# A macaron block on one core: the mixer chain split at the convolution, with four hid buffers and routing operands in PSUM

## The reference

```python
x = x + 0.5 * ffn(layernorm(x))
x = x + mixer(layernorm(x))
x = x + 0.5 * ffn(layernorm(x))       # the same weights as the first
```

## Time and profile before

| | us |
|---|---|
| median of 3 runs | 724.22 (724.0 to 727.43) |
| the profiled execution | 724.26 |
| its span, first to last instruction | 722.5 |
| PE busy / DVE busy / POOL busy / ACT busy | 668.6 / 580.9 / 480.9 / 420.2 |
| mean granted TensorE clock | 0.989 |

### The profile page before, as it was taken

The page is one execution under the profiler, slowest core; times in us unless marked ns, Lnnn a source line. Parts: engine busy times, 40 slices in busy tenths (PEclk is TensorE's granted clock), DMA queues, the critical chain, the costliest instruction groups (busy, mean ns, idle before and its releaser), DMA issues. The chain is left out here.

```text
span 722.5 us, 10391 instructions
## 1 busy us (share of the span) xinstructions
PE 668.6 (93%) x3016; PEld 524.4 (73%) x3016; DVE 580.9 (80%) x1543; ACT 420.2 (58%) x801; POOL 480.9 (67%) x714
## 2 busy tenths in 40 slices
PE   6589998988987999999999999999999899999996
PEld 5468776776766887767777787776778677777784
DVE  5787797788978788887897969988788887978663
ACT  4446655664665656566566565655665655665553
POOL 1147657765677766777567775777667776686775
PEclk9899999999999999999999999999999999999999
DMA  8492908308373290925719074461907346190550
GB/s 196 99 205 70 198 1 191 62 5 194 70 168 75 57 216 4 198 55 113 154 46 192 15 178 89 105 133 45 216 7 167 85 99 139 41 196 16 126 128 15
DMA packets 59994, 78.84 MB, mean 109 GB/s; under 512 B 7680, under 2 KB 27168, under 8 KB 59936
## 3 DMA queue, kind: packets, MB, share of 16 engines
q1 hardware_dynamic: 59408, 77.91, 49.8%
q10 hardware_dynamic: 528, 0.26, 0.2%
HBM read 75.01 MB, written 3.15 MB: 108 GB/s over the span
## 5 line engine op out<-in xcount | busy, mean ns | idle before, releaser
L479 POOL TENSOR_TENSOR hid_lo<-hid,hid_hi 128x256 fp32r<-128x256 f32 x544 | 392.1, 743 | 200.7 <-ACT hid_hi L576 200.0
L576 ACT ACTIVATE hid_hi<-hid 128x512 fp32r<-128x512 f32 x272 | 170.5, 627 | 118.5 <-DVE hid L725 117.3
L712 DVE TENSOR_TENSOR weighted<-gate_ps,raw 128x512 f32<-128x512 f32 x256 | 175.4, 685 | 68.7 <-ACT gate_ps L568 55.8
L568 ACT ACTIVATE gate_ps<-gate_ps 128x512 f32<-128x512 f32 x256 | 148.6, 580 | 105.5 <-PE gate_ps L982 103.0
L725 DVE TENSOR_TENSOR hid<-weighted,up_ps 128x512 f32<-128x512 f32 x256 | 174.8, 683 | 13.8 <-DVE weighted L712 0.5
L1025 PE MATMUL down_ps<-hid_hi,wt_hi 128*128 128x512 f32 x272 | 108.7, 400 | 6.7 <-ACT ffn_sb L580 6.7
L1028 PE MATMUL down_ps<-hid_lo,wt_hi 128*128 128x512 f32 x272 | 108.2, 398 | 0.8 <-POOL hid_lo L479 0.7
L1026 PE MATMUL down_ps<-hid_hi,wt_lo 128*128 128x512 f32 x272 | 107.9, 397 | 0.0
L980 PE MATMUL up_ps<-xT_hi,wt_hi 128*128 128x512 f32 x187 | 78.1, 417 | 12.5 <-DVE hid L725 12.2
L980 PE MATMUL gate_ps<-xT_hi,wt_hi 128*128 128x512 f32 x187 | 80.6, 431 | 4.1 <-DVE weighted L712 3.9
L982 PE MATMUL gate_ps<-xT_hi,wt_lo 128*128 128x512 f32 x187 | 74.8, 400 | 0.0
(11 more groups left out here) (140 smaller groups left out, 1082.7 us busy)
## 6 DMA issues: line engine op xcount, KB each, us to landing
raw<-wT_hbm SPq DMA_DIRECT2D x64, 640.0 KB, 13.3
raw<-wT_hbm SPq DMA_DIRECT2D x32, 512.0 KB, 7.7
raw<-wT_hbm SPq DMA_DIRECT2D x32, 256.0 KB, 3.9
x_res<-in_L_attn_x SPq DMA_DIRECT2D x8, 256.0 KB, 5.6
out_x<-x SPq DMA_DIRECT2D x8, 256.0 KB, 2.3
x_ln<-in_L_attn_x SPq DMA_DIRECT2D x7, 256.0 KB, 14.1
raw<-in_L_ffn_gate_w SPq DMA_DIRECT2D x4, 256.0 KB, 5.3
raw<-in_L_ffn_up_w SPq DMA_DIRECT2D x4, 256.0 KB, 4.9
```

The source lines that it names most:

```text
L479: last = nc.gpsimd.tensor_tensor(hid_lo[s][:, cols], hid[s][:, cols], hid_hi[s][:, cols].bitcast(F32), ALU.subtract)
L568: nc.scalar.activation(bank[:, :] if j else silu_sb[:, :], bank[:, :], ACT.Silu).then_inc(silu_done, 1)
L576: nc.scalar.activation(hid_hi[s][:, :], hid[s][:, :], ACT.Copy).then_inc(hid_hi_done, 1)
L712: V.tensor_tensor(weighted[j % 2][:, :], gate_ps[n % BANKS][:, :], wb[:, j - 1, :], ALU.mult)\
```

## The change

The ring of hid buffers gets a fourth member. Five small operands of the routing (16 columns each) are placed in free columns of the PSUM bank `routed`, where five others are already. The slot tables are redrawn: the chain is cut before the convolution. A unit (4, b) now carries layer norms 3 and 4 of block b+1 (`NORM4`), the chain of block b+2 up to the value's copy (`PROJECT`) and the first router of block b+3 (`PREPARE`). A unit (1, b) carries the convolution, recurrence and output projection of block b-1 (`MIXER`), the transpose and the second router of block b-2 (`XT4`, `ROUTE4`) and the output of block b-3. Stats and layer norm 1 of the next block (`NEXT`) come two to two and a half slots later, and the weights of both routers one slot later. PE issues down of tile 0 at slot 4 together with down of tile 1, instead of at slot 3. The tanh of the gate waits until the mixer's work on the block before is done.

```diff
--- before.py
+++ after.py
@@ -42,7 +42,7 @@
 
 ORDER = [(1, 0), (1, 1), (1, 2)] + [f for b in range(NBLK - 3) for f in ((4, b), (1, b + 3))]
 ORDER += [(4, NBLK - 3), (4, NBLK - 2), (4, NBLK - 1)]
-RING = 3
+RING = 4
 BANKS = 2
 NBATCH = 14
 
@@ -201,15 +201,15 @@
         best1 = sb("best1", [P, TT * NG])
         is_best = sb("is_best", [P, TT, E])
         others = sb("others", [P, TT, E])
-        n_best = sb("n_best", [P, TT * NG])
-        far_single = sb("far_single", [P, TT * NG])
+        n_best = routed[:, 388:388 + TT * NG]
+        far_single = routed[:, 404:404 + TT * NG]
         best1_tied = sb("best1_tied", [P, TT * NG])
-        best_other = sb("best_other", [P, TT * NG])
-        best2 = sb("best2", [P, TT * NG])
+        best_other = routed[:, 420:420 + TT * NG]
+        best2 = routed[:, 436:436 + TT * NG]
         gsum = sb("gsum", [P, TT, NG])
         gdiff = sb("gdiff", [P, TT, NG * NG])
         beats = sb("beats", [P, TT * NG, NG])
-        grank = sb("grank", [P, TT * NG])
+        grank = routed[:, 452:452 + TT * NG]
         gmask = sb("gmask", [P, TT * NG], I32)
         masked = sb("masked", [P, TT, E + TOP])
         top8 = sb("top8", [P, TT, 8])
@@ -286,40 +286,44 @@
         FIRST = {"norm 1": 0, "normalise 1": 0, "transpose 1": 2, "xT high 1": 2, "xT low 1": 2.5, "router 1": 3,
                  "logits 1": 3.5, "silu logits 1": 4, "route 1": (4.5, 5, 5.5, 6, 6.5, 7, 7.5, 8, 9, 9.5, 10),
                  "weights 1": 12}
-        NEXT = {"stats 1": 11.5, "meanvar 1": 12, "norm 1": 13, "normalise 1": 14}
+        NEXT = {"stats 1": 14, "meanvar 1": 14.5, "norm 1": 15, "normalise 1": 16}
         PREPARE = {"transpose 1": 1, "xT high 1": 1, "xT low 1": 1.5, "router 1": 2, "logits 1": 2.5,
-                   "silu logits 1": 3, "route 1": (4, 4.5, 5.5, 6, 6.5, 7, 8, 8.5, 9, 9.5, 10), "weights 1": 12}
-        CHAIN = {"copy ffn 1": 2, "transpose ffn 1": 3, "add ffn 1": 3.5, "stats 2": 4, "meanvar 2": 4,
-                 "norm 2": 4, "normalise 2": 5, "add ln_b": 9, "transpose 2": 7, "xT high 2": 7,
-                 "xT low 2": 7.5, "mixer gate": 9, "tanh gate": 9, "mixer value": 10, "copy value": 10,
-                 "conv": (11, 11.5, 12, 12.5, 13, 13.5), "y high": 14, "y low": 14,
-                 "mixer out": 16, "mixer sum": 16.5}
-        NORM4 = {"stats 3": 0, "meanvar 3": 0.5, "norm 3": 1, "normalise 3": 2, "scale 3": 3, "x2": 4.5, "stats 4": 5,
-                 "meanvar 4": 5, "norm 4": 6, "normalise 4": 7, "transpose 4": 14, "xT high 4": 14, "xT low 4": 14.5}
-        ROUTE4 = {"router 4": 1, "logits 4": 1.5, "silu logits 4": 2,
-                  "route 4": (2.5, 3.5, 5.5, 6, 6.5, 7, 8, 8.5, 9, 9.5, 10.5), "weights 4": 12}
+                   "silu logits 1": 3, "route 1": (4.5, 5, 5.5, 6.5, 7, 8, 8.5, 9.5, 10.5, 11, 12), "weights 1": 13}
+
+        PROJECT = {"copy ffn 1": 2, "transpose ffn 1": 3, "add ffn 1": 3.5, "stats 2": 4, "meanvar 2": 4,
+                   "norm 2": 4, "normalise 2": 5, "transpose 2": 7, "xT high 2": 7, "xT low 2": 7.5,
+                   "mixer gate": 9, "tanh gate": 9, "mixer value": 10, "copy value": 10, "add ln_b": 15}
+        MIXER = {"conv": (0, 0.5, 1, 2, 3, 3.5), "y high": 5, "y low": 5, "mixer out": 7, "mixer sum": 7.5,
+                 "stats 3": 13}
+        NORM4 = {"meanvar 3": 0, "norm 3": 0, "normalise 3": 1, "scale 3": 2, "x2": 12.5, "stats 4": 13,
+                 "meanvar 4": 13.5, "norm 4": 14, "normalise 4": 15}
+        XT4 = {"transpose 4": 1, "xT high 4": 1, "xT low 4": 1.5}
+        ROUTE4 = {"router 4": 2, "logits 4": 2.5, "silu logits 4": 3,
+                  "route 4": (4.5, 5, 5.5, 6.5, 7, 8, 8.5, 9.5, 10.5, 11, 12), "weights 4": 13}
         OUTPUT = {"copy ffn 4": 2, "transpose ffn 4": 3, "halve ffn": 3, "add ffn 4": 6}
 
 
         PREPARE2 = {"stats 1": 0.5, "meanvar 1": 0.5, "norm 1": 1, "normalise 1": 2, "transpose 1": 4, "xT high 1": 4,
                     "xT low 1": 4.5, "router 1": 5, "logits 1": 5.5, "silu logits 1": 6,
                     "route 1": (6.5, 7, 7.5, 8, 8.5, 9, 9.5, 10, 10.5, 11, 11.5), "weights 1": 13}
-        NORM4_0 = {**NORM4, "transpose 4": 8, "xT high 4": 8, "xT low 4": 8.5, "scale 3": 2, "x2": 3, "stats 4": 3.5,
-                   "meanvar 4": 3.5, "norm 4": 4, "normalise 4": 5}
+
+        WHOLE = {**PROJECT, "add ln_b": 9, "conv": (11, 11.5, 12, 12.5, 13, 13.5), "y high": 14, "y low": 14,
+                 "mixer out": 16, "mixer sum": 16.5}
+        NORM4_0 = {"stats 3": 0, "meanvar 3": 0.5, "norm 3": 1, "normalise 3": 2, "scale 3": 2, "x2": 3, "stats 4": 3.5,
+                   "meanvar 4": 3.5, "norm 4": 4, "normalise 4": 5, "transpose 4": 8, "xT high 4": 8, "xT low 4": 8.5}
         ROUTE4_0 = {"router 4": 9, "logits 4": 9.5, "silu logits 4": 10,
                     "route 4": (10.5, 11, 11.5, 12, 12.5, 13, 13.5, 14, 14.5, 15, 15.5), "weights 4": 16}
-
-        CHAIN1 = {**CHAIN, "transpose 2": 10, "xT high 2": 10, "xT low 2": 10.5, "mixer gate": 12, "tanh gate": 12,
-                  "mixer value": 13, "copy value": 13, "conv": (16, 16, 16.5, 16.5, 16.5, 16.5)}
-        REST1 = {}
-        for step in ("y high", "y low", "mixer out", "mixer sum"):
-            del CHAIN1[step]
-        REST1 = {"y high": 1, "y low": 1, "mixer out": 4, "mixer sum": 4.5, "stats 3": 10.5}
+        PROJECT1 = {**PROJECT, "transpose 2": 10, "xT high 2": 10, "xT low 2": 10.5, "mixer gate": 12,
+                    "tanh gate": 12, "mixer value": 13, "copy value": 13}
+
+        MIXER1 = {**MIXER, "stats 3": 10.5}
         NORM4_1 = {"meanvar 3": 10.5, "norm 3": 11, "normalise 3": 12, "scale 3": 13, "x2": 14.5,
                    "stats 4": 15, "meanvar 4": 15, "norm 4": 16, "normalise 4": 16}
-        XT4_1 = {"transpose 4": 1, "xT high 4": 1, "xT low 4": 1.5}
-        ROUTE4_1 = {"router 4": 2, "logits 4": 2.5, "silu logits 4": 3,
-                    "route 4": (3.5, 4, 5.5, 6, 6.5, 7, 8, 8.5, 9, 9.5, 10.5), "weights 4": 12}
+        PROJECT2 = {**PROJECT1, "normalise 2": 9, "add ln_b": 16}
+
+        MIXER6 = {**MIXER, "stats 3": 8}
+        NORM4_6 = {"meanvar 3": 8.5, "norm 3": 9, "normalise 3": 10, "scale 3": 11, "x2": 12.5, "stats 4": 13,
+                   "meanvar 4": 13, "norm 4": 14, "normalise 4": 15}
         NORM4_7 = {"stats 3": 0, "meanvar 3": 0, "norm 3": 0, "normalise 3": 1, "scale 3": 1, "x2": 2, "stats 4": 2.5,
                    "meanvar 4": 2.5, "norm 4": 3, "normalise 4": 4, "transpose 4": 6, "xT high 4": 6, "xT low 4": 6.5}
         ROUTE4_7 = {"router 4": 7, "logits 4": 7.5, "silu logits 4": 8,
@@ -330,23 +334,24 @@
             if (k, b) == (1, 0):
                 return at(FIRST, 1)
             if (k, b) == (1, 1):
-                return at(CHAIN, 0) + at(PREPARE2, 2)
+                return at(WHOLE, 0) + at(PREPARE2, 2)
             if (k, b) == (1, 2):
-                return at(NORM4_0, 0) + at(ROUTE4_0, 0) + at(CHAIN1, 1) + at(NEXT, 3)
+                return at(NORM4_0, 0) + at(ROUTE4_0, 0) + at(PROJECT1, 1) + at(NEXT, 3)
             if (k, b) == (4, 0):
-                return at(REST1, 1) + at(NORM4_1, 1) + at({**CHAIN, "add ln_b": 16}, 2) + at(PREPARE, 3)
-            if (k, b) == (1, 3):
-                return at(XT4_1, 1) + at(ROUTE4_1, 1) + at(NORM4, 2) + at(OUTPUT, 0) + at(NEXT, 4)
+                return at(MIXER1, 1) + at(NORM4_1, 1) + at(PROJECT2, 2) + at(PREPARE, 3)
+            if (k, b) == (1, NBLK - 1):
+                return (at(MIXER6, b - 1) + at(NORM4_6, b - 1) + at(XT4, b - 2) + at(ROUTE4, b - 2)
+                        + at(OUTPUT, b - 3))
             if (k, b) == (4, NBLK - 3):
-                return at(CHAIN, NBLK - 1) + at(ROUTE4, NBLK - 2)
+                return at(XT4, b + 1) + at(ROUTE4, b + 1) + at(WHOLE, b + 2)
             if (k, b) == (4, NBLK - 2):
-                return at(NORM4_7, NBLK - 1) + at(ROUTE4_7, NBLK - 1) + at(OUTPUT, NBLK - 3)
+                return at(NORM4_7, b + 1) + at(ROUTE4_7, b + 1) + at(OUTPUT, b - 1)
             if (k, b) == (4, NBLK - 1):
-                return at(OUTPUT, NBLK - 2)
+                return at(OUTPUT, b - 1)
             if k == 1:
-                return (at(NORM4, b - 1) + at(ROUTE4, b - 2) + at(OUTPUT, b - 3)
-                        + (at(NEXT, b + 1) if b < NBLK - 1 else []))
-            return at(CHAIN, b + 2) + at(PREPARE, b + 3)
+                return (at(MIXER, b - 1) + at(XT4, b - 2) + at(ROUTE4, b - 2) + at(OUTPUT, b - 3)
+                        + at(NEXT, b + 1))
+            return at(NORM4, b + 1) + at(PROJECT, b + 2) + at(PREPARE, b + 3)
 
         def due(steps, name, slot):
 
@@ -648,7 +653,8 @@
                         silu_logits(4, b)
                     for b in due(steps, "tanh gate", j):
                         act.wait_ge(mix_gate_ready, b + 1)
-
+                        if b > 0:
+                            act.wait_ge(mix, b * MIX)
                         nc.scalar.activation(gate_t[:, :], side[:, :], ACT.Tanh, scale=0.5)\
```

(4 more changed lines are left out.)

## The result

| | before | after |
|---|---|---|
| median | 725.03 (724.0 to 727.43) | 732.52 (731.76 to 734.33) |
| span of the profiled execution | 722.5 | 730.0 |
| mean granted TensorE clock | 0.989 | 0.974 |

The ratio is 1.0106, 95% interval 1.0086 to 1.0125: the change makes the kernel 1.1% slower. 709.5 us was forecast with a range up to 720; both are wrong, and so is the sign.

A forecast was written before the change was run, and what follows sets the result against it. PE was taken as the bound, but not always fed, stopping for late hid behind DVE's routing. Terms -12.5 - 3.2 - 3 - 0 - 2.5 - 1.5 + 8 = -14.7 from 724.3 gave 709.5 us, range 698 to 720.

The forecast's parts named there:

- part 7: Fuller early slots of (1, b), unit ends and normalise 3 in (4, b): 8 us given back, bounds 0 to 30.
- the 41 forecast: Expected length of a (4, b) unit after the change: near 41 us, from 43.0.
- One of the prediction's own signs of being wrong: Listed beforehand: PE waiting for xT_lo or the router more than 2 us a unit would show the forecast wrong.
- DVE's allowance: PE may run two tiles ahead, so 1.9 us of lateness of hid were estimated to cost nothing.
- Part 1: Routing operands in PSUM shorten L786, L788 and L807 and PE's stops for hid: 12.5 us saved, bounds 0 to 16.8.
- part 2: Two half-clock stretches behind PE stops go, 1.6 us each: 3.2 us saved, bounds -1.6 to 3.2.
- free nothing: Rival: PSUM operands free nothing, parts 1 and 2 are 0; 725 us, chance 0.10.
- Parts 3 and 6: (1, b) units: normalise 3 leaves slot 2, 3 us saved; xT high 4 leaves the ends, 1.5 us saved.
- Part 4: down 0 one slot later and ring of 4: worth 0, the stop moving from L1025 to L1033.
- Part 5: The conv leaves the end of (1, 2) and late (4, b) slots: 2.5 us saved, bounds 0 to 4.9.
- The burst decides: Rival: DVE enters (1, b) units already late, so added conv work stops PE; 731.6 us, chance 0.07.
- The price of a PSUM operand: Rival: small PSUM operands cost 0.1 us for each of five operations; 714.6 us, chance 0.03.

The follow-up runs named there:

- both neighbours early: Changed kernel with norm 3 at slot 14 of the unit before and layer norm 1 in its old slots, normalise 3 still at slot 1: 713.79 us.
- normalise 1 early: Changed kernel with stats 1 to normalise 1 back in their old slots (11.5 to 14), normalise 3 still at slot 1: 724.55 us.
- the last two mended versions: Changed kernel, old NEXT slots, beat_at in PSUM, (4, 0) norms earlier; normalise 3 at slot 3: 709.9 us; then slot 1, norm 3 at 14: 706.17 us.
- norm 3 early: Changed kernel with meanvar 3 and POOL's norm 3 at slot 14 of the unit before, normalise 3 still at slot 1: 726.02 us.

## Why the prediction was wrong

The forecast was 23.0 us too low. **The step that failed is in part 7**: "In the (4, b) units normalise 3 (1.64) comes before xT high 1 at slot 1, and PE's router waits for xT low: 0.3 in four." The place was named and the size of that step by itself was right, 0.27 with both neighbours early. Wrong was to take it by itself.

In the same three slots the change also moved normalise 1 to slot 16 (1.65 us of ACT) and norm 3 to slot 0 of POOL, behind `hid_lo`. Each of the three waits for the other engine's last one, so they add up to 3.3 us and bring a stretch at half clock, worth 1.6 us (with normalise 1 early alone, 43.7 in a unit with one, 42.1 in the one without). Both neighbours moved back, the four units give 4 x (44.8 - 40.3) = 18.0 us. Against the 41 forecast the four are 15 us too long, and (4, 0), below, some 7: about the whole error. One of the prediction's own signs of being wrong, PE waiting for `xT_lo` more than 2 us a unit, is what came.

The prediction had both facts: that a late normalise "delays the tiles ahead" is in part 7, and the earlier trace rows has ACT waiting 1.84 us for POOL's scale. It put them to the ends of units and to DVE's allowance, and not to the router, which has little of it. PE wants `xT_lo` one slot after the transposes, and in (4, 2) of the kernel before it was ready 0.6 us ahead (the end of L742 at 345.86, the router at 346.43), where `hid` may be 1.9 us late.

Part by part:

- **Part 1, PSUM operands.** Direction and the three durations right (174 to 179 ns), the size not: alone 5.4 us instead of 15.7 with part 2. In the (1, b) units the stops hid a second limit, POOL's scale and ACT's normalise 4, so the next late thing was `weighted`, as the rival "free nothing" had it; the wait for POOL's reads went on to L795 (in the changed kernel L801 and L806, 395 and 524 ns). In the changed kernel they are worth 12.0. The allowance of 1.9 us stands, though the terms given for its 3.0 us add up to 3.5: in the trace `hid` ends 3.0 us after the gate's first matmul where nothing is late.
- **Part 2, clock.** The price was too high: (1, 5) with its stretch took 42.3 us before, (1, 4) and (1, 6) without one 41.9, so 0.4 and not 1.6 there. The two old stretches went, four came at the router's stops and others in (4, 0) and (1, 3): 0.974 instead of 1.00.
- **Parts 3 and 6.** Right: no `ffn_sb` wait is left in (1, 3) to (1, 7), and (1, 4) to (1, 6) take 40.7.
- **Part 4.** 0 forecast, -1.6 us measured for both edits together; the two stops moved on to transpose ffn as said. Which of the two brings the 1.6 was not tried.
- **Part 5.** Opposite in sign. -2.5 forecast, +4.6 in (4, 0): normalise 1 now stands ahead of `wT`, 2 to 2.8 us, and the conv had stood where DVE waits for the broadcast anyway. The move itself need not lose: in the last two mended versions, where it stays, (4, 0) takes 45.1, 2.9 below before.
- **The rivals.** "The burst decides" has the right total, 731.6, and not the mechanism: the conv's slots in (1, b) are no loss; of its place only the ACT block at the end of the units before had a part. The price of a PSUM operand is not there.

The total of that rival is luck. The chance of 0.07 on slower was too small because all the terms that could go wrong were weighed one at a time.

## What to carry to other kernels

When steps are moved to new slots, write down for each in-order engine what stands ahead of the first instruction that PE waits for, and follow it back across the engines; three small delays on ACT, POOL and ACT again are one chain and cannot be priced one by one. Look first at operands that PE wants soonest after they are made: late `hid` had 1.9 us of allowance, late `xT_lo` 0.6. And when a wait is taken away, ask which instruction meets it next, and which other chain would have been late at the same place.

## What the runs showed of the hardware

- Stops of nearly equal length are not always followed by half clock. The router's stop of 1.87 us (norm 3 early) was, in (4, 1) and (4, 4), and was not in (4, 2) and (4, 3); that of 2.10 (normalise 1 early) in three units of four; that of 3.3 in all four. By the same measure the kernel before had half clock behind stops of 1.9 in (1, 5) and 2.1 in (1, 3), and none behind one of 2.0 at the end of (1, 2). It may be why the time scatters (not shown): the kernel with 1.87 ran from 721.62 us, at a mean clock of 0.980, to 731.88, at 0.969. The two kinds, behind the stop of (4, 1) and of (4, 2), norm 3 early:

```profile
266.90:273.70 6.80, 6.80 (x25) 5.92 (x25) 4.51 (x8) 1.71 (x4) 4.05 (x5) 0.50 1.07 220
354.00:357.40 3.40, 3.40 (x19) 2.78 (x18) 3.21 (x6) 2.30 (x5) 2.60 (x3) 1.00 1.05 217
```

- A DVE operation of 64 columns with two SBUF inputs took 0.94 us beside a POOL add, and 213 ns on the mean with all five operands back in SBUF, where the earlier L792 and L794 of the same routing averaged 612 and 547.
- A PSUM operand cost a 16-column operation nothing that shows: 174 to 179 ns, against 0.18 us for the one in the earlier trace rows with two SBUF inputs and no wait.
